# Four layers on one NeuronCore: the first attention's weights, bias and keys in another order

## What is computed

```python
q = split(x @ Wq.T + bq); k = split(x @ Wk.T + bk); v = split(x @ Wv.T + bv)   # 16 heads of 16
phi(y) = (exp(y @ orf.T / d**0.25 - sum(y*y) / (2*sqrt(d))) + 1e-6) / 8          # 64 features a head
kv, ksum = phi(k).T @ v, phi(k).sum(rows)                                       # per batch
x = layernorm(x + (phi(q) @ kv / (phi(q) @ ksum)) @ Wo.T + bo)
```

## Time and profile before

| | us |
|---|---|
| median of 3 runs | 4896.46 |
| profiled execution, its own time | 4890.4 |
| its span | 4888.6 |
| TensorE busy | 4515.6 (92%) |
| DVE busy | 3507.1 (72%) |
| ACT busy | 2784.2 (57%) |
| POOL busy | 1059.7 (22%) |

### The profile page before, as it was taken

The page is one execution under the profiler, slowest core; times in us unless marked ns, Lnnn a source line. Parts: engine busy times, 40 slices in busy tenths (PEclk is TensorE's granted clock), DMA queues, the critical chain, the costliest instruction groups (busy, mean ns, idle before and its releaser), DMA issues. The chain is left out here.

```text
span 4888.6 us, 65492 instructions
## 1 busy us (share of the span) xinstructions
PE 4515.6 (92%) x25456; PEld 1682.4 (34%) x25456; DVE 3507.1 (72%) x3872; ACT 2784.2 (57%) x5253; POOL 1059.7 (22%) x1003
## 2 busy tenths in 40 slices
PE   5787898699998999999999999999999999999896
PEld 2444443466664222222222222222222232222374
DVE  2344445698787877888777888877888988888232
ACT  1222222233332677888777777777777757788611
POOL 5323232335442112000112110111111011100213
PEclk7899999899998899999999999999999999999998
DMA  2010000001221223112224222233222221222233
GB/s 94 21 58 18 27 14 13 10 14 61 69 82 51 67 100 130 48 65 71 81 94 131 64 80 83 71 113 98 79 83 74 67 68 44 84 69 78 76 117 59
DMA packets 233082, 333.23 MB, mean 68 GB/s; under 512 B 37026, under 2 KB 174308, under 8 KB 230724
## 3 DMA queue, kind: packets, MB, share of 16 engines
q1 hardware_dynamic: 229892, 321.19, 20.0%
q0 software_dynamic: 2880, 7.87, 0.9%
HBM read 221.50 MB, written 98.04 MB: 65 GB/s over the span
## 5 line engine op out<-in xcount | busy, mean ns | idle before, releaser
L1498 DVE TENSOR_REDUCE mx<-ps 128x1 f32<-128x1024 f32 x2048 | 2407.2, 1220 | 437.5 <-PE ps L690 434.3
L1265 ACT ACTIVATE Pb<-ps 128x512 f32<-128x512 f32 x4096 | 2201.4, 596 | 501.0 <-PE ps L690 496.6
L690 PE MATMUL ps<-QS,KS 98*128 98x512 bf16 x4096 | 1252.5, 387 | 13.9 <-ACT Pb L1265 6.4
L690 PE MATMUL ps<-Pb,VA 128*32 128x512 f32 x8192 | 1099.5, 609 | 0.1
L690 PE MATMUL ps<-KM,QM 64*128 64x512 bf16 x4096 | 662.3, 391 | 57.4 <-DVE mx L1498 55.3
L690 PEld LDWEIGHTS ps<-QS,KS 98*128 98x128 bf16 x4096 | 261.7, 98 | 1082.4 <-ACT Pb L1265 889.4
L690 PEld LDWEIGHTS ps<-KM,QM 64*128 64x128 bf16 x4096 | 179.5, 93 | 615.2 <-issue 350.3
L1827 POOL CAST mrow<-mres 16x128 bf16<-16x128 f32 x64 | 18.2, 285 | 1352.7 <-ACT mres L1094 1352.7
L690 PEld LDWEIGHTS ps<-Pb,VA 128*32 128x32 f32 x8192 | 161.6, 108 | 400.8 <-issue 399.8
L690 PE MATMUL ps<-wdT,hT 128*128 128x256 f32 (+1 forms) x768 | 195.4, 397 | 20.3 <-DVE X L1483 15.4
L1378 DVE TENSOR_TENSOR phi<-ps,ns 128x1024 f32<-128x1024 f32 x64 | 78.2, 1222 | 189.4 <-PE ps L690 189.3
(11 more groups left out here) (251 smaller groups left out, 4511.1 us busy)
## 6 DMA issues: line engine op xcount, KB each, us to landing
QM<-qd SPq DMA_DIRECT2D x128, 256.0 KB
KM<-kd SPq DMA_DIRECT2D x128, 256.0 KB
qd<-parts SPq DMA_DIRECT2D x96, 256.0 KB, 2.8
kd<-parts SPq DMA_DIRECT2D x96, 256.0 KB, 2.8
QS<-qd SPq DMA_DIRECT2D x64, 384.0 KB
KS<-kd SPq DMA_DIRECT2D x64, 384.0 KB
vdr<-vst SPq DMA_DIRECT2D x64, 256.0 KB, 2.9
den<-rd SPq DMA_DIRECT2D x64, 256.0 KB
```

The costliest lines, as they stand in the source:

```text
L690: return eng.matmul(out, a, b, start=start, stop=stop, skip_group_check=skip)
L1265: eng.activation(Pb[(u - 1) % 9], o, ACT.Exp, bias=0.0, scale=0.25).then_inc(act_A, 1)
L1498: eng.tensor_reduce(mx4[qc % 2][:, 4 * i + q, h:h + 1], o, AX, ALU.max).then_inc(dve_D, 1)
```

## The change

Four things change, all in the first attention.

1. *Weights.* They are no longer woven into batch 0's keys but into the queries of batches 0 and 1 (rate 45 instead of 34), with empty steps between them. POOL's four rounding operations are now four steps of their own (`wb`). The zero row is made from the last 256 columns of `W`, which alone are zeroed.
2. *Bias.* POOL adds `bo` to a chunk of X in that chunk's `nq` step. The loads become steps of their own (`rl`): two after each chunk of batch 0's keys, the upper eight behind the weights at the end of batch 1's queries.
3. *Keys.* The products k, v and kn of chunk C+1 are issued between the phi steps of chunk C (`ahead`), within a batch. Rate 46 instead of 40.
4. *Banks.* For batch 0 the keys' second product and kn use bank 4, and the two values products banks 5 and 6, in place of bank 0 for all. Later batches stay in bank 0.

Besides, SP's first loads and DVE's first operations stand in another order.

```diff
-KRATE = 40
-WRATE = 34
+KRATE = 46
+WRATE = 45
 def keys_order(b):
+    made = lambda C: [("k", C, 0), ("k", C, 1), ("v", C, 0), ("v", C, 1), ("kn", C)]
+    for step in made(4 * b):
+        yield [step]
     for C in range(4 * b, 4 * b + 4):
-        for ht in range(2):
-            yield [("k", C, ht)]
-        for g in range(2):
-            yield [("v", C, g)]
+        ahead = made(C + 1) if C % 4 < 3 else []
         for j in range(4):
             n = 4 * C + j
-            yield [("kn", C)] * (j == 0) + [("phi", n)] + [("kv", n - 1)] * (n % 16 > 0)
+            yield [("phi", n)] + [("kv", n - 1)] * (n % 16 > 0)
+            if ahead:
+                yield ahead[j:j + 1] if j < 3 else ahead[3:]
+        if b == 0:
+            yield [("rl", 2 * C), ("rl", 2 * C + 1)]
...
-        yield [("fq", C)] + ([("ap0", stats)] if stats is not None else []) + [("nq", C)]
+        yield [("fq", C)] + ([("ap0", stats)] if stats is not None else []) + [("nq", C), ("res", C)]
...
     for m in range(3):
-        yield ([("w0",)] if m == 0 else []) + [("wl", m)]
+        yield [("wl", m)]
+        yield from [[]] * 4
         yield [("wq", m)]
+        yield from [[]] * 2
         yield [("wa", m)]
+        for i in range(4):
+            yield []
+            yield [("wb", m, i)]
+        yield from [[]] * 2
         for a in range(6):
             yield [("wt", m, a)]
+            yield []
...
-    plan.extend(("res", C) for C in range(8))
     w = weights_order()
-    woven(plan, (keys_order(0), 34), (w, WRATE))
+    together(plan, keys_order(0))
+    plan.append(("w0",))
     for b in range(3):
         k = keys_order(b + 1)
         woven(plan, (queries_order(b, range(4), 0), 49), (k, KRATE), (w, WRATE))
         together(plan, k)
-        if b == 0:
+        if b == 1:
             together(plan, w)
-            plan.extend(("res", C) for C in range(8, CH))
+            plan.extend(("rl", C) for C in range(8, CH))
...
+    k_bank = lambda C, ht: bank(4 if C < 4 and ht else 0)
+    v_bank = lambda C, g: bank(5 + g if C < 4 else 0)
...
         def k(C, ht):
...
-            if ht:
+            if C < 4:
+                if ht and C:
+                    w.wait_ge(act_kn, at["kn", C - 1])
+                elif C:
+                    w.wait_ge(act_k, at["k", C - 1, 0])
+            elif ht:
                 w.wait_ge(act_k, at["k", C, 0])
             elif C % 4:
                 w.wait_ge(act_kn, at["kn", C - 1])
...
-        def wa(m):
+        def wb(m, i):
+            x = 4 * m + i
             w.wait_ge(act_wq, m + 1)
-            rounded(wxn, wc, wsc, pool_wq, 4 * m)
+            w.wait_ge(pool_wq, x)
+            if i == 0:
+                d = eng.tensor_scalar(wc, wc, LEAST, None, ALU.max)
...
         def setup():
-            load(ident, t["ident"]).then_inc(ld_ident, 16)
+            load(bqk["k"], t["bk"]).then_inc(ld_k, 16)
             load(flat(WT["k"]), t["WkT"]).then_inc(ld_k, 16)
             fetch(0, xk[0], ld_xk[0])
-            fetch(1, xk[1], ld_xk[1])
-            load(bqk["k"], t["bk"]).then_inc(ld_k, 16)
             load(flat(WT["v"]), t["WvT"]).then_inc(ld_v, 16)
             load(bvo["v"], t["bv"]).then_inc(ld_v, 16)
-            load(n8, t["n8"]).then_inc(ld_n, 16)
-            load(flat(nq), t["nq"]).then_inc(ld_n, 16)
...
+            load(n8, t["n8"]).then_inc(ld_n, 16)
+            load(flat(nq), t["nq"]).then_inc(ld_n, 16)
+            fetch(1, xk[1], ld_xk[1])
+            load(ident, t["ident"]).then_inc(ld_ident, 16)
...
-        def res(C):
+        def rl(C):
             if C == 8:
                 w.wait_ge(pe_wt, 18)
```

More of the change, by code:

```diff
@@ L702, in k @@
                 w.wait_ge(act_kn, at["kn", C - 1])
-            elif C:
+            else:
                 w.wait_ge(dve_kvt, C // 4)
-            mm(bank(0), WT["k"][:, 0, ht * P:(ht + 1) * P], xk[i][:, 0, :], True, False)
-            mm(bank(0), WT["k"][:, 1, ht * P:(ht + 1) * P], xk[i][:, 1, :], False, True).then_inc(pe_k, 1)
+            mm(o, WT["k"][:, 0, ht * P:(ht + 1) * P], xk[i][:, 0, :], True, False)
+            mm(o, WT["k"][:, 1, ht * P:(ht + 1) * P], xk[i][:, 1, :], False, True).then_inc(pe_k, 1)
         def v(C, g):
@@ L710, in v @@
             w.wait_ge(ld_v, 32)
-            if g:
+            if C < 4:
+                if C:
+                    w.wait_ge(dve_v, at["v", C - 1, g])
+            elif g:
                 w.wait_ge(dve_v, at["v", C, 0])
@@ L716, in v @@
                 for k in range(2):
-                    d = mm(bank(0)[:, 256 * j:256 * j + 256], xk[i][:, k, (2 * g + j) * P:(2 * g + j + 1) * P], WT["v"][:, k, :], k == 0, k == 1)
+                    d = mm(v_bank(C, g)[:, 256 * j:256 * j + 256], xk[i][:, k, (2 * g + j) * P:(2 * g + j + 1) * P], WT["v"][:, k, :], k == 0, k == 1)
             d.then_inc(pe_v, 1)
@@ L722, in kn @@
             w.wait_ge(ld_n, 32)
-            w.wait_ge(dve_v, at["v", C, 1])
+            if C >= 4:
+                w.wait_ge(dve_v, at["v", C, 1])
             for j in range(4):
                 for ht in range(2):
-                    d = mm(bank(0)[:, 16 * j + 8 * ht:16 * j + 8 * ht + 8], k2[C % 2][:, ht, j * P:(j + 1) * P], n8)
+                    d = mm(k_bank(C, 1)[:, 16 * j + 8 * ht:16 * j + 8 * ht + 8], k2[C % 2][:, ht, j * P:(j + 1) * P], n8)
             d.then_inc(pe_kn, 1)
@@ L731, in phi_ @@
             w.wait_ge(act_k, at["k", C, 1])
-            w.wait_ge(dve_setup, 2)
+            w.wait_ge(dve_setup, 4)
             if n:
@@ L784, in q @@
                 w.wait_ge(dve_kvt, 4)
+            else:
+                w.wait_ge(act_kn, 4)
             mm(bank(b4), WT["q"][:, 0, ht * P:(ht + 1) * P], xq_[i][:, 0, :], True, False)
@@ L798, in pq @@
             w.wait_ge(act_q, at["q", C, 1])
-            w.wait_ge(dve_setup, 2)
+            w.wait_ge(dve_setup, 4)
+            if C == 0:
+                w.wait_ge(dve_v, at["v", 3, 1])
             if ht or g:
@@ L1100, in k @@
                 w.wait_ge(pe_phi, 4 * (C - 1))
-            eng.activation(kT[C % 2][:, ht, :], bank(0), ACT.Identity, bias=bqk["k"][:, ht:ht + 1], scale=1.0).then_inc(act_k, 1)
+            eng.activation(kT[C % 2][:, ht, :], k_bank(C, ht), ACT.Identity, bias=bqk["k"][:, ht:ht + 1], scale=1.0).then_inc(act_k, 1)
         def kn(C):
@@ L1106, in kn @@
                 w.wait_ge(dve_phi, 4 * (C - 1))
-            copy(flat(ns[C % 2]), bank(0)[:, 0:64]).then_inc(act_kn, 1)
+            copy(flat(ns[C % 2]), k_bank(C, 1)[:, 0:64]).then_inc(act_kn, 1)
         def phi_(n):
@@ L1347, in setup @@
             eng.memset(Wblk, 0.0).then_inc(dve_setup, 1)
+            for v in va:
+                eng.memset(v, 1.0).then_inc(dve_setup, 1)
             w.wait_ge(ld_orf, 128)
             eng.tensor_scalar(Wblk, Wblk, 0.5, None, ALU.mult).then_inc(dve_setup, 1)
[L1350 to L1354, removed]
+            eng.memset(W[:, 1280:1536], 0.0).then_inc(dve_setup, 1)
         def wq(m):
@@ L1363, in v @@
             w.wait_ge(ld_v, 32)
-            w.wait_ge(dve_setup, 4)
+            w.wait_ge(dve_setup, 3)
             if C > 1:
@@ L1367, in v @@
             for j in (0, 1):
-                d = eng.tensor_tensor(va[C % 2][:, 2 * g + j, :, 0:16], bank(0)[:, 256 * j:256 * j + 256].rearrange("p (a b) -> p a b", a=16),
+                d = eng.tensor_tensor(va[C % 2][:, 2 * g + j, :, 0:16], v_bank(C, g)[:, 256 * j:256 * j + 256].rearrange("p (a b) -> p a b", a=16),
                                       bvo["v"].rearrange("p (a b) -> p a b", a=16), ALU.add)
@@ L1683, in yn @@
             norm_apply(xr[g][:, 5 * f:5 * f + 5, :], ("yp", g, f), 5)
-        stages = {"setup": setup, "w0": w0, "wq": wq, "v": v, "phi": phi_, "kvt": kvt, "nq": nq_, "num": num, "o": o, "st0": st0,
+        stages = {"setup": setup, "wq": wq, "v": v, "phi": phi_, "kvt": kvt, "nq": nq_, "num": num, "o": o, "st0": st0,
                   "ap0": ap0, "phase1": phase1, "qx": qx, "up": up, "qa": qa, "qb": qb, "qc": qc, "da": da, "st1": st1,
@@ L1728, in rounded @@
             eng.tensor_tensor(x, x, sc.unsqueeze(2).to_broadcast(list(x.shape)), ALU.mult).then_inc(own, 1)
-        def wa(m):
+        def wb(m, i):
+            x = 4 * m + i
             w.wait_ge(act_wq, m + 1)
-            rounded(wxn, wc, wsc, pool_wq, 4 * m)
+            w.wait_ge(pool_wq, x)
+            if i == 0:
+                d = eng.tensor_scalar(wc, wc, LEAST, None, ALU.max)
+            elif i == 1:
+                d = eng.tensor_tensor(wxn, wxn, wc, ALU.add)
+            elif i == 2:
+                d = eng.tensor_tensor(wxn, wc, wxn, ALU.subtract)
+            else:
+                v = wxn.rearrange("p (b k) -> p b k", k=16)
+                d = eng.tensor_tensor(v, v, wsc.unsqueeze(2).to_broadcast(list(v.shape)), ALU.mult)
+            d.then_inc(pool_wq, 1)
         def q(C, ht):
@@ L1868, in ys @@
                     in_=xr[g][:, b, :], in_offset=None, bounds_check=8191, oob_is_err=False).then_inc(st_fin, 16)
```

(6 more changed lines are left out.)

2 lines of the change are left out of this document (1 added, 1 removed).

## The result

The changed kernel takes 4855.91 us, the median of four runs (4851.50 to 4867.53), against 4896.44 before: a ratio of 0.9921, 95% interval 0.9908 to 0.9933. It is faster by 40 us, and not by the 93 that were forecast. The profiled execution of the changed kernel was its slowest (4867.53, span 4865.7), so the comparison is made inside the first attention: it ends at 837.9 us and ended at 871.9, 34 us earlier. What lies behind the first attention took between 4009.7 and 4027.8 us in the 17 profiled executions, in no order that follows the changes; it was longest in the changed kernel's.

What follows compares the result with a forecast made beforehand. TensorE bounds the kernel, with holes in the first attention from weights' work and POOL's bias additions. 4890.4 - 93 (keys) - 18 (hole) + 3 (additions, loads) + 20 (weights) = 4802, forecast as 4803 us; range 4781 to 4838.

Steps and rivals of the forecast that it cites:

- sign of failing: First attention: the prediction fails if batches with weights take over 210 us, or the keys' stage ends after 110.
- The first batch's keys: Batch 0's stage before the first query product: ends at 96.4 us against 189.7, 93 us gained, bounds 84 to 98.
- The 17.8 us hole: Second woven batch: TensorE's wait behind POOL's run of eight bias additions goes, 17.8 us.
- The last batch's 3 us: Last batch's two query streams: thinner cover for additions and a possible load wait cost 3 us (0 to 12).
- Bias chunk by chunk: Woven batches: sixteen additions of 2.35 us are covered by slack in POOL's queue; with the hole gone, 15 us gained.
- Rival 1: Chunks' nq step: DVE waits for each addition, pq products 2.35 us late in 15 chunks; 35 us more, 4838; chance 0.08.
- Order and rates: Woven batches: key steps at rate 46 lengthen the query tail to 12.7 steps; net nothing, 7 us a batch either way.
- Rival 2: Queries left alone: the longer tail costs 7 us in each of three woven batches, 4824; chance 0.14.
- The weights: Weights' steps strewn over batches 0 and 1 cost 20 us, from 5 to 64.
- POOL's 5: Batches 0 and 1: twelve single POOL operations for the weights cost 0.4 us a block, 5 us.
- DVE's 6: Batches 0 and 1: one DVE block of 4.85 us per matrix makes the chain 2 us late each, 6 us.
- the transposes' 10: Batches 0 and 1: the weights' transposes take 8 us, plus 2 us waiting in bank 7, 10 us.

Runs made afterwards that it cites:

- e12: The kernel before with only the bias added chunk by chunk, behind the second num, all loads where they were; 4865 us, ratio 0.9954.
- e5: The changed kernel with the bias addition moved from the nq step to the empty step behind the second num; ratio 0.9883.
- e2: The changed kernel with the keys of batches 1 to 3 in their old order, still at rate 46; ratio 0.9910.
- e3: The changed kernel with the keys of batches 1 to 3 in their old order and rate 40, addition left at nq; 4850 us, ratio 0.9903.
- e7: The changed kernel with the bias addition behind the second num and the keys' rate 40, keys still ahead; 4854 us, ratio 0.9911.
- e6: The changed kernel with old key order in batches 1 to 3, rate 40 and the bias addition behind the second num; ratio 0.9838.
- e8: The changed kernel with rate 40, addition behind the second num, and kn issued with its chunk's first phi in batches 1 to 3; 4818 us, ratio 0.9841.

## Why the prediction was right or wrong

By stage, gains in the first attention (minus: a loss):

| | forecast | measured |
|---|---|---|
| keys of batch 0 | 93 | 91.6 |
| first woven batch | -10 | -23.8 |
| second | 17.8 - 10 | -11.5 |
| third | 0 | -19.7 |
| last | -3 | -2.6 |
| sum | 88 | 34.0 |

The prediction's own sign of failing, weights' batches over 210 us, came true (211.5 and 216.4). Its last sum has a slip too: 4802 was worked out for a profiled execution 6 us under the median, so the median should have been forecast at 4808, and 4803 is 5 us too low.

- **The first batch's keys** were right in mechanism and size, each step within 2 us: phi at 23, three chunks at TensorE's own rate, the last at 3.30 us a phi.
- **The 17.8 us hole** was right: e12 shows 19.6 in the second batch with that part alone.
- **The last batch's 3 us** is right by luck. It was put down to a thinner cover and a load; but with the addition moved (e5) the batch takes 100.7 us instead of 105.1 and is 1.8 shorter than before, so the loss was the same blocking as below.
- **"Bias chunk by chunk": the step that the addition is covered failed.** I asked whether POOL's own queue has room, and it has. I did not follow whom it blocks on DVE. Rival 1 had the mechanism, with 35 us and a chance of 0.08; measured is 23.4 at the change's rate, and 36.0 at a rate of 40. My argument against it was that nq and ACT's copy pass before the split, so that the addition would be over by then. But POOL comes to the addition only behind a phi scaling of the keys: it starts at 588.96, and the cast it blocks at 589.25. By the Trainium skill, "SBUF — State Buffer", section "Who interferes with whom", casts are among the operations that can take the shared port pair; the cast's 2.34 us beside POOL's 2.35 and 0.42 without it agree.
- **"Order and rates": the step "net nothing" failed.** In the third batch rate and the kn step cost 6.5 and 7.0 us, once the addition is moved. The tail without keys is 43.6 us and not the 36 that I summed, with a clock of 0.84; and I left out that kn now stands in one step with the second values product of the same bank, where it used to stand a step later. Rival 2 named the tail with 7 us a batch: 6.5 in the third batch here, 4.6 in the old order (e2 and e3). Over all three batches the rate of 46 alone is no loss with keys ahead, as e7 is longer than e5; it is the rate and kn's place together that cost 18.1.
- **The weights**: forecast 20. The two batches with weights are 14.3 us over twice the third in the changed kernel, but 37.7 in e6; in e8 they are 36.2 over the kernel before without its hole (187.7 and 187.1). That the loose tail hid part of them is my reading and not shown. All three terms were too small: POOL's 5 measured 8.5 to 12, DVE's 6 measured 11 to 13, and the transposes' 10 measured 13 to 18 with ACT's part, which I had put at nothing.
- The 54 us short, along the path from the changed kernel over e5 to e8, are then: addition 23.4, order and rate 18.1 (batches 0 to 2 of e5 against e8), weights 16.2 more than forecast in the tight kernel (36.2 for 20), keys 1.4, less 5.2 for the last and third batch, which came out shorter in e8 than forecast. Another path would share them out otherwise.

What remains open: why kn's place costs most in the first batch at rate 40 (220.8 in e7, 208.0 in e8). The windows say where the 12.8 us are: TensorE is busy for 184.2 us at a clock of 0.90 against 175.5 at 0.93, and it waits 6.2 us for the addition of the values, 4.4 the longest, against 0.3. What lowered the clock there isn't shown. In batches 0 and 1 of the changed kernel TensorE is busy for 179.7 and 180.5 us, 12 more than before; the 36 transposes are 7.3 of both together, and no kernel here separates the clock from the waits that go before.

## What to carry to other kernels

A block moved to an idle engine has to be checked against what it blocks on the others, and not only against its own queue: here sixteen additions of 2.35 us on POOL, 22% busy, cost 23 to 36 us in the place where DVE's casts ran beside them. When streams are woven by rates, the tail of the one that outlasts the others is a cost of its own, and a change of rate also changes which steps stand side by side; judge it by a stage that the rest of the change doesn't touch, and then by all of them: here the shorter tail was worth 6.5 us in one batch and cost 11.8 in all. Two steps that share a PSUM bank should not stand next to each other when another engine empties the bank in between (0.9911 against 0.9841 of the kernel before, e7 and e8).

## What was not expected of the hardware

Waits of 2.25 and 4.07 us in a stretch otherwise full of products were each followed by products at the lower clock (3.50 us for a phi of 1.98, 3.76 for a product of the same width). The length of one wait doesn't decide it: the dense part of the third batch in the kernel before also has waits of up to 2.2 us, and its clock is 0.99; in the changed kernel it is 0.94. Slower products made up 13 of the third batch's 20 us. The steps to e5, e7 and e8 gave back 4.0, 5.5 and 3.8 us of TensorE's busy time, so no single kind of wait accounts for it; which waits lowered the clock is not separated.
